# A two-layer kernel (depthwise-separable convolution, then a spiral scan): the pointwise product as three fp32r products, taken in the tick of the 512-wide layer

## The chip, the cores and the metric

The kernel runs on one core of a Trainium2 chip. The metric is the device time of one execution in microseconds (us); lower is better. TensorE is called PE below, its weight loads PEld, VectorE DVE, ScalarE ACT, GpSimd POOL, SyncE SP. A row of the trace is one instruction or a group of them.

## The reference

`x` is 32 images of 56 x 56 positions with 256 channels, float32. Layer 0 is a depthwise 3 x 3 convolution with dilation 2 on relu(x), then a pointwise 256 x 256 product, with biases and a normalization. Layer 1 walks the positions on a spiral, in place, and needs both a position's own value and the mean of its neighbours.

```
h = relu(x)
h = depthwise_conv(h, dw_kernel, dilation 2) + dw_bias
h = h @ pw_kernel + pw_bias                       # 256 -> 256
g = h * inv + (beta - moving_mean * inv)          # inv = gamma / sqrt(var + eps)
for p in spiral:                                  # one after the other, in place
    u = concat(g[p], mean of the neighbours of p) # 512 wide
    y = tanh(u @ w1 + b1) @ w2 + b2               # hidden layer, 512 wide
    g[p] = g[p] + y * w_y
```

## The kernel before

The work has two parts in time. In the first (up to about 3170 us of the profiled execution) everything is computed that does not depend on the scan's results: the layer-0 value of every position, and for every position the part of `u @ w1` that needs layer 0 alone. Both are written to DRAM in the order of the scan (`s_x`, `s_pre`). In the second part the scan reads them back tile by tile, adds the terms of the scan, and stores the output. The change is in the first part.

The first part handles 112 rows (56 image rows, for each half of the 32 images). A row is 7 tiles of 128 (position, image) pairs, so there are 784 tiles. All engines follow one order written out by hand: a loop over ticks, one tile for each tick. The tick of a step is its constant plus the tile's number. Per tick, and modulo 7 for what is done once for a row:

- SP loads a row of `x` (896 KB).
- PE transposes it in two of the seven ticks (7 pieces of 128 x 128, L861). ACT applies relu into `relu_rows` (L563, twice a row) and does the centre tap into `dw_rows` (L552, twice for a pair of rows).
- DVE does the other eight taps (L676, in a regular row eight instructions of 128 x 1792), the sums of neighbours (L689, L702, L712), and the low parts `u_lo` of the split operand (L726, four for a row).
- The split: an operand is rounded to fp32r (`u_hi`, on ACT, L541, four for a row: own values and neighbour sums, for tiles 0 to 3 and 4 to 6) and the rest is kept in `u_lo`. The first two of the four 128-deep slices are the row's own `dw_rows` values, the other two the neighbour sums.
- PE does the pointwise product of a tile in plain fp32 from `dw_rows` with `pw` (L872: two matmuls of 256 columns, four instructions in the trace) into banks 6 and 7. Six ticks later (`HID_LAG`) it does the 512-wide layer of that tile: for each of four slices hi*hi, hi*lo, lo*hi (L888, L889, L890), twelve fp32r matmuls of 512 columns into banks 4 and 5.
- ACT copies the two results out, one tick after each (`eo` from the 512-wide layer, L517, then `xo`, L523), and at the end of the tick writes the bias into the bank just emptied (L572). The pointwise product accumulates on that bias, so PE waits for L572 ahead of the product of the next tile but one. `eo` and `xo` have four slots each: ACT waits until the transfer of four tiles before has landed.
- POOL issues two indirect transfers in a tick, one after the other: `s_x` (L458, 128 KB) and `s_pre` (L464, 256 KB).

At the end of the first part SP waits for the last of both transfers before it reads `s_pre` back. In the setup DVE folds the normalization into `pw` (L613) and `bias_all` (L617), and PE transposes `pw` for the merged weights.

## Time and profile before

| what | value |
| --- | --- |
| three runs | 4768.79, 4776.31, 4791.13 us (median 4776.31) |
| profiled execution, its own time | 4755.92 us |
| its span, first to last instruction | 4754.1 us |
| mean granted TensorE clock | 0.993 |
| busy share of the span | PE 94%, PEld 70%, DVE 84%, ACT 54%, POOL 72% |
| first part | up to about 3170 us |

Matmuls are pipelined and their ends are modelled: consecutive matmul rows overlap, so the time of one is read from the distance of the starts, and a busy PE is not PE at its peak. "issue" in a wait means that nothing shown by the profile was waited for. Spans on POOL are rough.

### The profile page before, as it was taken

What the parts mean: (1) busy time and instruction counts of PE and PEld (TensorE: products, weight loads), DVE (VectorE), ACT (ScalarE), POOL (GpSimd) and SP (SyncE); (2) the same over time, 40 slices, a digit from 0 to 9 for tenths busy, and PEclk for the clock granted to TensorE, in tenths of its full rate; (3) what the DMA queues carried; (4) which work ended last, traced back from release to release, by engine and by line L of the source; (5) the groups of instructions that cost most, each with busy time, mean ns of one, the idle gap of its engine ahead of it and who ended that gap; (6) DMA issues with size and microseconds to landing.
All of it is one profiled execution on the core that took longest, in us unless ns stands there. A gap on an engine that the chain in (4) does not pass through costs nothing.

```text
span 4754.1 us, 62034 instructions
## 1 busy us (share of the span) xinstructions
PE 4491.0 (94%) x19609; PEld 3350.7 (70%) x19609; DVE 3981.0 (84%) x5685; ACT 2551.0 (54%) x4523; POOL 3445.8 (72%) x2478
## 2 busy tenths in 40 slices
PE   4999999999999999999999999998888899999889
PEld 3888878888888888888878888864444445555556
DVE  7888888888888788888888888738888888898884
ACT  4566656666666666665656666444344444444552
POOL 1888888888887788888888888756666666665542
PEclk8999999999999999999999999999999999999999
DMA  4344444444444444444444444359999998888751
GB/s 101 124 139 134 133 134 140 132 135 138 131 138 138 129 138 134 131 142 131 132 132 140 132 136 130 151 178 318 303 299 320 296 301 291 287 273 256 209 176 51
DMA packets 394994, 835.52 MB, mean 176 GB/s; under 512 B 76848, under 2 KB 178480, under 8 KB 394544
## 3 DMA queue, kind: packets, MB, share of 16 engines
q1 hardware_dynamic: 249008, 417.52, 31.4%
q0 software_dynamic: 143408, 411.26, 23.2%
q8 instruction: 163, 2.67, 0.2%
q10 hardware_dynamic: 2256, 2.77, 0.2%
q14 instruction: 159, 1.30, 0.1%
HBM read 420.17 MB, written 425.85 MB: 178 GB/s over the span
## 4 chain that ended last, share of the span: by engine, by line
PE 61%; DVE 12%; issue 10%; ACT 7%; DMA 5%; POOL 4%; SPq 0%; DVEq 0%; POOLq 0%; ACTq 0%
PE psum L888 13%; PE psum L890 13%; PE psum L889 13%; PE psum L872 13%; DVE psum L752 5%; DMA out<-dw_rows 4%; DVE dw_rows L760 3%; ACT relu_rows L563 3%; POOL out L476 3%; PE psum L861 3%; PE psum L928 2%; PE psum L912 1%; PE psum L901 1%; DMA s_pre<-eo,wave_idx 1%; PE psum L919 1%
## 5 line engine op out<-in xcount | busy, mean ns | idle before, releaser
L676 DVE SCALAR_TENSOR_TENSOR dw_rows<-relu_rows,taps,dw_rows 128x1792 f32<-128x1792 f32 x872 | 1803.4, 2079 | 6.2 <-issue 5.2
L464 POOL DMA_INDIRECT s_pre<-eo,wave_idx x784 | 1327.0, 1693 | 249.7 <-issue 224.2
L458 POOL DMA_INDIRECT s_x<-xo,wave_idx x784 | 1215.2, 1550 | 377.5 <-issue 233.8
L476 POOL DMA_INDIRECT out<-dw_rows x897 | 899.8, 1003 | 677.2 <-issue 401.3
L888 PE MATMUL psum<-w_hi,u_hi 128*128 128x512 f32 x3136 | 1383.4, 441 | 0.0
L890 PE MATMUL psum<-w_hi,u_lo 128*128 128x512 f32 x3136 | 1231.8, 393 | 0.0
L889 PE MATMUL psum<-w_lo,u_hi 128*128 128x512 f32 x3136 | 1224.7, 391 | 0.0
L517 ACT ACTIVATE eo<-psum 128x512 f32<-128x512 f32 x784 | 468.1, 597 | 1218.6 <-PE psum L890 1160.9
L901 PE MATMUL psum<-dw_rows,ident 128*128 128x512 f32 x1666 | 885.0, 613 | 98.1 <-DVE near L752 74.7
L872 PE MATMUL psum<-pw,dw_rows 128*128 128x256 f32 x3136 | 818.8, 384 | 61.6 <-ACT psum L572 44.9
L581 ACT ACTIVATE psum<-psum 128x512 f32<-128x512 f32 x897 | 522.0, 582 | 545.8 <-PE psum L912 283.7
L752 DVE CUSTOM_DVE_ANT_0 psum<-psum,dw_rows,b_col 128x512 f32<-128x512 f32 x897 | 676.4, 754 | 112.8 <-ACT psum L581 106.4
L872 PEld LDWEIGHTS psum<-pw,dw_rows 128*128 128x128 f32 x3136 | 570.7, 190 | 183.1 <-issue 103.3
L890 PEld LDWEIGHTS psum<-w_hi,u_lo 128*128 128x128 f32 x3136 | 589.7, 188 | 137.9
L889 PEld LDWEIGHTS psum<-w_lo,u_hi 128*128 128x128 f32 x3136 | 592.2, 189 | 122.5
L888 PEld LDWEIGHTS psum<-w_hi,u_hi 128*128 128x128 f32 x3136 | 591.8, 189 | 117.9
L912 PE MATMUL psum<-u_hi 128*128 128x512 f32 x897 | 620.1, 691 | 43.1 <-ACT u_hi L590 33.7
L726 DVE TENSOR_TENSOR u_lo<-near,u_hi 128x1024 fp32r<-128x1024 f32 x224 | 243.7, 1088 | 384.6 <-ACT u_hi L541 257.3
L760 DVE SCALAR_TENSOR_TENSOR dw_rows<-dw_rows,near 128x256 f32<-128x256 f32 x897 | 434.0, 484 | 126.7 <-DMA out<-dw_rows 80.5
L901 PEld LDWEIGHTS psum<-dw_rows,ident 128*128 128x128 f32 x1666 | 269.0, 189 | 336.0 <-issue 317.0
L563 ACT ACTIVATE relu_rows<-psum 128x896 f32<-128x896 f32 x224 | 414.6, 1855 | 20.7 <-DMA dwb_c<-L_conv_dw_bias 10.6
L572 ACT ACTIVATE psum<-bias_all 128x256 f32<-128x256 f32 x782 | 332.5, 425 | 5.6
(90 smaller groups left out, 3913.6 us busy)
## 6 DMA issues: line engine op xcount, KB each, us to landing
dw_rows<-s_pre SPq DMA_DIRECT2D x615, 256.0 KB
x_tok<-x SPq DMA_DIRECT2D x112, 896.0 KB
dw_rows<-s_x SPq DMA_DIRECT2D x615, 128.0 KB
dw_rows<-s_pre SPq DMA_DIRECT2D x169, 192.0 KB
dw_rows<-s_x SPq DMA_DIRECT2D x169, 96.0 KB
out<-dw_rows POOLq DMA_INDIRECT x897
s_x<-xo,wave_idx POOLq DMA_INDIRECT x784
s_pre<-eo,wave_idx POOLq DMA_INDIRECT x784
```

Source lines behind the costliest of these rows:

```text
L458: pool.indirect_dma_start(s_x, bass.IndirectOffsetOnAxis(wave_idx[:, n:n + 1], 0), xo[:, n % XO_SLOTS, :], None, bounds_check=TILES * P - ...
L464: pool.indirect_dma_start(s_pre, bass.IndirectOffsetOnAxis(wave_idx[:, n:n + 1], 0), eo[:, n % EO_SLOTS, :], None, bounds_check=TILES * P - 1,
L476: pool.indirect_dma_start(out_rows, bass.IndirectOffsetOnAxis(store_idx[:, c:c + 1], 0), o_t[:, c % OUT_SLOTS, :], None, bounds_check=OUT_ ...
L676: dve.scalar_tensor_tensor(out=dst, in0=pair_rows(relu_rows, k + ky - 1, c, 2 * kx * NB), scalar=taps[:, c, 3 * ky + kx:3 * ky + kx + 1], ...
L752: dve.tensor_tensor_reduce(out=bank, in0=bank, in1=w2_row, scale=1.0, scalar=b2_col[:, 0:1], op0=ALU.mult, op1=ALU.add, accum_out=y_of(c)) ...
L760: dve.scalar_tensor_tensor(out=o_t[:, c % OUT_SLOTS, :], in0=wy_row, scalar=y_of(c), in1=x_t[:, c % XT_SLOTS, :], op0=ALU.mult, op1=ALU.ad ...
L872: last = pe.matmul(bank, dw_rows[:, R % D_SLOTS, c, NB + P * t:NB + P * (t + 1)], pw[:, c, :], start=False, stop=c == CK - 1, skip_group_c ...
L888: pe.matmul(bank, hi, w_hi[:, k, :], start=k == 0, stop=False)
L889: pe.matmul(bank, hi, w_lo[:, k, :], start=False, stop=False)
L890: last = pe.matmul(bank, lo, w_hi[:, k, :], start=False, stop=k == 2 * CK - 1)
L901: pe.matmul(psum[:, c % BANKS, :], ident[:, :], pre_t[:, c % PRE_SLOTS, :], start=True, stop=False).then_inc(passed, 1)
L912: pe.matmul(psum[:, c % BANKS, :], s_rows[:, part, :], v_sel[:, row, :], start=False, stop=True, skip_group_check=by_act(c)).then_inc(pre_ ...
```

## The change

- `pw` is split in the setup into `pw_hi` and `pw_lo` (two instructions on DVE). It is itself loaded into a part of the `relu_rows` ring that is not in use yet.
- The pointwise product takes the operands of the 512-wide layer: for the two slices that hold the row's own values, `u_hi`*`pw_hi`, `u_hi`*`pw_lo`, `u_lo`*`pw_hi`, six fp32r matmuls of 256 columns. Each stands behind the matmul of the 512-wide layer that has the same stationary operand, in the same tick; the two fp32 matmuls are gone.
- The pointwise product is thereby six ticks later. One constant, `TILE_LAG`, replaces `HID_LAG` on PE, ACT and POOL. The number of ticks is unchanged.
- Waits for `xp_ready` where `dw_rows` is freed become waits for `lo_ready`, since the product does not read `dw_rows` any more.

```diff
-                n = tick - ROW_AT
-                if 0 <= n < TILES1:
-                    R, t = divmod(n, T)
-                    pe.wait_ge(conv_step, conv_done_for(R // 2))
-                    pe.wait_ge(xp_filled, n + 1)
-                    bank = xp_bank(n)
-                    for c in range(CK):
-                        last = pe.matmul(bank, dw_rows[:, R % D_SLOTS, c, NB + P * t:NB + P * (t + 1)], pw[:, c, :],
-                                         start=False, stop=c == CK - 1, skip_group_check=True)
-                    last.then_inc(xp_ready, 1)
-
-                n = tick - ROW_AT - HID_LAG
+                n = tick - ROW_AT - TILE_LAG
                 if 0 <= n < TILES1:
...
                     pe.wait_ge(lo_ready, 4 * R + 2 * part + 2)
+                    pe.wait_ge(xp_filled, n + 1)
                     if n >= 2:
                         pe.wait_ge(hid_copied, n - 1)
-                    bank = psum[:, 4 + n % 2, :]
+                    hid, point = psum[:, 4 + n % 2, :], xp_bank(n)
                     for k in range(2 * CK):
                         hi, lo = u_hi[:, slot, k, at:at + P], u_lo[:, slot, k, at:at + P]
-                        pe.matmul(bank, hi, w_hi[:, k, :], start=k == 0, stop=False)
-                        pe.matmul(bank, hi, w_lo[:, k, :], start=False, stop=False)
-                        last = pe.matmul(bank, lo, w_hi[:, k, :], start=False, stop=k == 2 * CK - 1)
+                        pe.matmul(hid, hi, w_hi[:, k, :], start=k == 0, stop=False)
+                        if k < CK:
+                            pe.matmul(point, hi, pw_hi[:, k, :], start=False, stop=False, skip_group_check=True)
+                        pe.matmul(hid, hi, w_lo[:, k, :], start=False, stop=False)
+                        if k < CK:
+                            pe.matmul(point, hi, pw_lo[:, k, :], start=False, stop=False, skip_group_check=True)
+                        last = pe.matmul(hid, lo, w_hi[:, k, :], start=False, stop=k == 2 * CK - 1)
+                        if k < CK:
+                            last_point = pe.matmul(point, lo, pw_hi[:, k, :], start=False, stop=k == CK - 1,
+                                                   skip_group_check=True)
+                    last_point.then_inc(xp_ready, 1)
                     last.then_inc(hid_ready, 1)
```

The rest of it, cut: on POOL and ACT the two blocks of a tick become one, with the order of the instructions kept.

```diff
 # POOL
-                n = tick - ROW_AT - 2
+                n = tick - ROW_AT - TILE_LAG - 2
                 if 0 <= n < TILES1:
                     pool.wait_ge(xp_copied, n + 1)
...
-                n = tick - ROW_AT - HID_LAG - 2
-                if 0 <= n < TILES1:
                     pool.wait_ge(hid_copied, n + 1)
 # ACT, centre tap
-                        act.wait_ge(xp_ready, 2 * T * (k - 2))
                         act.wait_ge(lo_ready, 4 * 2 * (k - 2))
 # DVE, setup
             link(dve.tensor_copy(bias_all[:, :], cst))
             assert done[0] == SETUP_CST
+            link(dve.tensor_copy(pw_hi[:, :, :], pw))
+            link(dve.tensor_tensor(pw_lo[:, :, :], pw, pw_hi[:, :, :].bitcast(f32), ALU.subtract))
 # SP and DVE, end of the first part
-            sp.wait_ge(xp_ready, TILES1)
+            sp.wait_ge(lo_ready, 4 * ROWS)
-            dve.wait_ge(xp_ready, TILES1)
+            dve.wait_ge(lo_ready, 4 * ROWS)
```

## Rows read from the trace of the kernel before

**Rows 1.** The page's busy time, and two stretches (busy us and instructions of PE, PEld, DVE, ACT, POOL; PEclk, DMA).
```profile
PE 4491.0 (94%) x19609; PEld 3350.7 (70%) x19609; DVE 3981.0 (84%) x5685; ACT 2551.0 (54%) x4523; POOL 3445.8 (72%) x2478
...
160.00:460.00 300.00, 297.91 (x1386) 246.43 (x1385) 265.56 (x166) 182.81 (x308) 253.05 (x155) 1.00 0.43 135
...
2560.00:2860.00 300.00, 297.94 (x1386) 246.42 (x1385) 265.46 (x166) 185.91 (x309) 250.84 (x154) 1.00 0.43 135
```

**Rows 2.** Groups of instructions, 460 to 2860 us (busy, mean ns; idle before, releasers).
```profile
L464 POOL DMA_INDIRECT s_pre<-eo,wave_idx x613 | 1065.6, 1738 | 190.5 <-issue 174.5 <-ACT xo L523 16.0
L458 POOL DMA_INDIRECT s_x<-xo,wave_idx x614 | 935.8, 1524 | 208.7 <-issue 187.4 <-ACT xo L523 20.8 <-ACT eo L517 0.6
L889 PEld LDWEIGHTS psum<-w_lo,u_hi 128*128 128x128 f32 x2448 | 461.8, 189 | 95.3
L517 ACT ACTIVATE eo<-psum 128x512 f32<-128x512 f32 x612 | 365.4, 597 | 927.4 <-PE psum L890 893.9 <-DMA s_pre<-eo,wave_idx 32.2 <-issue 0.6
```

**Rows 3.** Timeline of PE, ticks of the steady part (start, duration).
```profile
514.38 1.03 PE L872 MATMUL psum<-pw,dw_rows 128*128 128x256 f32 x4
517.99 1.02 PE L872 MATMUL psum<-pw,dw_rows 128*128 128x256 f32 x4
521.95 1.10 PE L872 MATMUL psum<-pw,dw_rows 128*128 128x256 f32 x4 [0.17 <-ACT psum L572]
```

**Rows 4.** Timeline of ACT, one regular row of 7 tiles, from tick to tick.
```profile
1428.56 0.60 ACT L517 ACTIVATE eo<-psum 128x512 f32<-128x512 f32 x1
1448.62 0.84 ACT L541 ACTIVATE u_hi<-dw_rows 128x768 fp32r<-128x768 f32 x1
1452.24 0.60 ACT L517 ACTIVATE eo<-psum 128x512 f32<-128x512 f32 x1 [2.50 <-PE psum L890]
1455.87 0.60 ACT L517 ACTIVATE eo<-psum 128x512 f32<-128x512 f32 x1
```

**Rows 5.** Timeline of PE and ACT at the end of the first part.
```profile
3134.96 1.02 PE L872 MATMUL psum<-pw,dw_rows 128*128 128x256 f32 x4
3138.59 1.02 PE L872 MATMUL psum<-pw,dw_rows 128*128 128x256 f32 x4
3166.89 0.60 ACT L517 ACTIVATE eo<-psum 128x512 f32<-128x512 f32 x1 [2.12 <-PE psum L890]
3169.61 0.60 ACT L517 ACTIVATE eo<-psum 128x512 f32<-128x512 f32 x1 [2.12 <-PE psum L890]
```

**Rows 6.** Timeline of PE in the scan: short fp32 matmuls, two instructions each.
```profile
4506.57 0.38 PE L919 MATMUL psum<-ident,near 128*124 128x128 f32 x2
4506.79 0.38 PE L920 MATMUL psum<-near 128*124 128x128 f32 x2
```

**Rows 7.** Timeline of DVE, the same row.
```profile
1446.09 1.23 DVE L726 TENSOR_TENSOR u_lo<-near,u_hi 128x1024 fp32r<-128x1024 f32 x1 [2.80 <-issue]
1449.50 0.96 DVE L726 TENSOR_TENSOR u_lo<-dw_rows,u_hi 128x768 fp32r<-128x768 f32 x1 [0.19 <-ACT u_hi L541]
1450.38 4.13 DVE L676 SCALAR_TENSOR_TENSOR dw_rows<-relu_rows,taps,dw_rows 128x1792 f32<-128x1792 f32 x2
1455.30 2.07 DVE L676 SCALAR_TENSOR_TENSOR dw_rows<-relu_rows,taps,dw_rows 128x1792 f32<-128x1792 f32 x1
```

**Rows 8.** Timeline of POOL beside it.
```profile
1444.44 0.98 POOL L458 DMA_INDIRECT s_x<-xo,wave_idx  x1 [0.31 <-issue]
1445.73 0.97 POOL L464 DMA_INDIRECT s_pre<-eo,wave_idx  x1 [0.30 <-issue]
1450.46 0.97 POOL L458 DMA_INDIRECT s_x<-xo,wave_idx  x1 [0.30 <-issue]
1455.66 2.56 POOL L464 DMA_INDIRECT s_pre<-eo,wave_idx  x1 [0.30 <-issue]
```

**Rows 9.** Timeline of DVE (setup) and POOL (last transfer of the first part).
```profile
38.58 0.42 DVE L620 COPY eo<-psum 128x256 f32<-128x256 f32 x1 [2.13 <-PE psum L823]
3170.98 0.97 POOL L464 DMA_INDIRECT s_pre<-eo,wave_idx  x1 [1.74 <-ACT eo L517]
```

More of the change, by code:

```diff
@@ L33 @@
 ROW_AT = 21
-HID_LAG = 6
+TILE_LAG = 6
 FIRST_TICK = -20
@@ L38 @@
 TILES1 = ROWS * T
-LAST_TICK = TILES1 - 1 + ROW_AT + HID_LAG + 3
+LAST_TICK = TILES1 - 1 + ROW_AT + TILE_LAG + 3
 CONV_TAPS = [(0, 0), (0, 1), (0, 2), (1, 0), (1, 2), (2, 0), (2, 1), (2, 2)]
@@ L268, in build @@
         w_lo = sb("w_lo", [P, 2 * CK, HID], f32r)
-        pw = sb("pw", [P, CK, C])
+        pw_hi = sb("pw_hi", [P, CK, C], f32r)
+        pw_lo = sb("pw_lo", [P, CK, C], f32r)
         ident = sb("ident", [P, P])
@@ L333, in build @@
         tmp_r = u_hi[:, 0, 0:2, :]
+        pw = relu_rows[:, R_SLOTS - 1, :, PADX * NB:PADX * NB + C]
         x_in = [sem(f"x_in{i}") for i in range(X_SLOTS)]
@@ L486, in _ @@
                 (mva, bc(mvar, C)), (gam, bc(gamma, C)),
-                (pw[:, :, :], pwk.rearrange("a b (k p) n -> p (a b k) n", p=P)),
+                (pw, pwk.rearrange("a b (k p) n -> p (a b k) n", p=P)),
                 (pwb_r, bc(pwb, C)), (mme, bc(mmean, C)), (bet, bc(beta, C)), (wy_s, bc(wy, C)),
@@ L511, in _ @@
                         act.activation(xp_bank(n), bias_all[:, :], ACT.Copy).then_inc(xp_filled, 1)
-                n = tick - ROW_AT - HID_LAG - 1
+                n = tick - ROW_AT - TILE_LAG - 1
                 if 0 <= n < TILES1:
@@ L517, in _ @@
                     act.activation(eo[:, n % EO_SLOTS, :], psum[:, 4 + n % 2, :], ACT.Copy).then_inc(hid_copied, 1)
-                n = tick - ROW_AT - 1
-                if 0 <= n < TILES1:
                     act.wait_ge(xp_ready, n + 1)
@@ L566, in _ @@
                                    ACT.Relu).then_inc(row_ready, 1)
-                n = tick - ROW_AT - 1
+                n = tick - ROW_AT - TILE_LAG - 1
                 if 0 <= n < TILES1 - XP_BANKS:
@@ L863, in _ @@
                     last.then_inc(x_transposed, 1)
-                n = tick - ROW_AT
-                if 0 <= n < TILES1:
-                    R, t = divmod(n, T)
-                    pe.wait_ge(conv_step, conv_done_for(R // 2))
-                    pe.wait_ge(xp_filled, n + 1)
-                    bank = xp_bank(n)
-                    for c in range(CK):
-                        last = pe.matmul(bank, dw_rows[:, R % D_SLOTS, c, NB + P * t:NB + P * (t + 1)], pw[:, c, :],
-                                         start=False, stop=c == CK - 1, skip_group_check=True)
-                    last.then_inc(xp_ready, 1)
-                n = tick - ROW_AT - HID_LAG
+                n = tick - ROW_AT - TILE_LAG
                 if 0 <= n < TILES1:
@@ L984 @@
 SETUP_CST = 1 + 6 + CK + 3 + 1
-SETUP_T = SETUP_CST + 4
+SETUP_T = SETUP_CST + 2 + 4
 SETUP_W = SETUP_T + 2 * CK
```

## The prediction

> **What bounds the kernel now.** The page comes first: PE is busy 94% of the span; in the first part, 784 ticks of one tile each, where the change lies, it is busy 298 of every 300 us at full granted clock [rows 1]. Two views are then needed, because matmul rows overlap and the busy share says little.
>
> The timeline of PE gives the tick from start to start of the pointwise product: 3.61 us (514.38 to 517.99), then 3.96 with a short wait for ACT's bias write L572 [rows 3]. ACT's copies show the whole row of 7 tiles: 1428.56 to 1455.87, 27.31 us [rows 4]. Every row has it: a row has 7 x (12 + 4) + 14 = 126 matmul instructions, and the first and the last of eight stretches of 300 us (two of the others are a little short) have 1386 of them, 11.0 rows [rows 1]. Apart from the start and the last four rows that makes about 105. Of the seven ticks, two carry transposes on top, and one is set by ACT: from L517 at 1452.24 ACT does its copies, an L541, the relu and the bias write without a pause and reaches the next L517 3.63 us later [rows 4], while PE waits. The other six are PE's own.
>
> The groups of instructions show a second engine that the busy share hides. From 460 to 2860 us POOL's two transfers take 1065.6 + 935.8 us, and 174.5 + 187.4 us more are the fixed 0.30 us between two of them; on ACT it waits some 37 us [rows 2]. So POOL is occupied 98.5% of 2400 us: it is as close to the limit as PE. ACT in turn waits 32.2 us for landed `s_pre` transfers, that is, POOL already pushes back at times [rows 2].
>
> Why POOL takes that long is read by laying its timeline beside DVE's. A transfer takes 0.97 us where it starts while DVE is idle or has started within 0.08 us (1445.73; 1450.46 against L676 at 1450.38), and otherwise ends 0.85 us after the DVE instruction that runs: 1455.66 + 2.56 = 1458.22, and the L676 of 1455.30 ended at 1457.37 [rows 7, 8]. [...]
>
> **The change part by part.** *PE.* At the end of the first part ticks with the pointwise product take 3.63 us (3134.96 to 3138.59), those without it 2.72 (3166.89 to 3169.61) [rows 5]. So the fp32 pair costs 0.91. The six new matmuls: 2.72 / 12 = 0.227 us for 512 columns, half for 256, 0.113; times six 0.68. A bound from below: short fp32 instructions, each with a weight load of its own, follow each other at 0.22 / 2 = 0.11 [rows 6], six make 0.66. From above: a load row lasts 0.189 [rows 2], and if a short matmul can't hide it, six cost 1.13. I take 0.113, because in rows 6 a load of this length stands behind a matmul as short as these. Gain 0.91 - 0.68 = 0.23 a tick.
>
> [...]
>
> On PE alone: six ticks of a row at 0.23 make 1.4 us (the tick that ACT sets gives nothing), 27.3 to 25.9.
>
> *POOL.* It still has 14 transfers in a row, and gets no faster. Count what DVE allows now. A row has ten instructions of about 2 us (eight L676, L689, L702), four L726 and the short L712. With 0.30 + 0.97 between two transfers, each of the ten lets through one, ending 0.85 behind it; so does the L726 that ends DVE's long wait. An L726 of 0.96 is passed over, except the one with 0.19 us of idle time ahead (the transfer at 1450.46). The long wait of 2.80 lets two through freely (1444.44, 1445.73). Sum 10 + 1 + 1 + 2 = 14, exactly what a row needs [rows 7, 8]. If PE is faster, it is these waits of DVE that shrink, because DVE's own work stays. How far? The second free transfer starts 0.85 + 0.30 + 0.97 + 0.30 = 2.4 us after the end of the last instruction, and the one after it, 1.27 later, must find the L726 of 1.23 us still running: 3.7 - 1.2 = 2.5. So 2.80 can become about 2.5. After that POOL falls behind, the four slots fill, ACT waits for a landed transfer, and PE and DVE wait for ACT. This gives 0.3 us of a row; the small wait can lend a few hundredths too, so I take 0.35: row 26.95, 105 x 0.35 = 37 us.
>
> *Ends.* Rows 108 to 111, without convolution on DVE, are PE's: 7 x 0.23 x 4 = 6 us gained. The last six ticks now carry the pointwise product: 6 x 0.68 = 4 lost. The last `s_pre` stood 1.37 us behind its `eo` (3169.61 to 3170.98 [rows 5, 9]); now an `s_x` of 0.30 + 0.97 and a part of the copy of `xo` come between, some 1.6 lost. The two DVE instructions of the setup, at most 2 x 0.42 each by the 256-column copy, fall into the 2.13 us that DVE waits there for PE [rows 9]; without that cover they cost 1.7. ACT's and SP's changed waits are for counters that are reached earlier. Together about 0.
>
> *Moved steps.* Six ticks later for the product moves L523, L572 and `s_x` too, but in ACT and POOL the order within a tick and the number are as before, so nothing new queues behind them. PE's wait for the bias stood at the head of a tick and still does.
>
> Sum: 4755.92 - 37 = 4719. The median of the runs shown, 4776.31, is 20 us above the profiled execution; predicted 4739.
>
> **Rivals.** *POOL doesn't bind* (transfers find gaps that my count misses): the row goes to 25.9 to 26.2, 1.1 to 1.4 x 105 = 115 to 147 us, on the median's base 4630 to 4660. For it: a wait of DVE of only 0.19 us ahead of a short L726 buys a whole transfer [rows 7, 8], and there are two such L726 in a row; against it: the 98.5%.
>
> *POOL's rate is the row.* Neither of the two waits lends anything; what PE gains, ACT waits for landed transfers. 4776, at most 15 less.
>
> *POOL loses a slot: slower.* The 0.19 us ahead of the L726 at 1449.50 come from ACT's L541 of the next tick, at 1448.62 [rows 4, 7], which follows PE. If PE's tick is 0.23 shorter, this wait is gone, the transfer at 1450.46 is blocked for the rest of an L676, and a row has 13. The fourteenth needs 1.27 us more of DVE idle time in the long wait: 2.5 + 1.27 = 3.8 for 2.8, less the 0.19, row 27.3 + 0.8 = 28.1, 0.8 x 105 = 84 us more, 4860. It decides as soon as the tick gains more than 0.19. Against it: once ACT waits for transfers, its ticks are apart again and the small wait returns by itself.
>
> [...]
>
> **How the numbers follow.** A difference under about 0.5% (24 us) can't be told from none in a measurement of this kernel. Forecast, row 26.6 to 27.07: 0.36. POOL doesn't bind: 0.20. POOL's rate is the row: 0.24. Lost slot: 0.16. Not short: 0.04. Faster 0.56, same 0.24, slower 0.20. The range leaves out the last case and a part of the outer two: 4640 to 4840. The forecast's own range is 4700 to 4750.
>
> **What would show it.** In the changed kernel: matmul rows of 256 columns 0.11 us ahead of the next (right) or 0.19 and more (not short). Ticks of 3.4 us on PE where nothing waits. The row between two L517 seven ticks apart: 26.95; 25.9 if POOL doesn't bind; 28.1 if it lost a slot. L517 waiting for `s_pre` in nearly every row, with POOL's wait for ACT gone, is the mark of POOL as the bound; L517 waiting for PE throughout would make the forecast wrong. DVE's long wait at 2.5, and whether the small one ahead of the 128x768 L726 is still there, tells forecast from lost slot.

## The result and the profile after

The changed kernel takes 4832.89 us (median; 4829.29 to 4835.48), the kernel before beside it 4777.1: a ratio of 1.0113 with an interval of [1.0091, 1.0134]. It is slower, where the prediction forecast 4739. The profiled execution has a span of 4833.7 us (before: 4754.1), 1.7% more. That is more than the medians give, because the kernel before was slower in its timed executions here (4768.79 to 4791.13) than in its profiled one (4755.92). Beside the experiments below its median is 4747.12 to 4763.51. So ratios of different experiments can be off against each other by about 0.6%, and where it matters the rows of the profiles are compared too. One execution of the grouped kernel below took 12346.51 us at a granted clock of 0.365; it is not in its ratio.

First the page's busy time, then the view of stretches: the same two as in [rows 1], with 460 to 2860 us between them (columns as there).

```profile
PE 4424.6 (92%) x21177; PEld 3342.9 (69%) x21177; DVE 3981.3 (82%) x5687; ACT 2541.5 (53%) x4523; POOL 3511.5 (73%) x2478
...
160.00:460.00 300.00, 285.23 (x1502) 239.70 (x1501) 261.64 (x164) 176.97 (x300) 252.87 (x151) 0.98 0.42 132
2560.00:2860.00 300.00, 285.17 (x1489) 240.50 (x1488) 256.03 (x160) 178.09 (x301) 252.42 (x152) 0.97 0.42 134
460.00:2860.00 2400.00, 2281.93 (x11998) 1921.75 (x11997) 2048.90 (x1274) 1432.35 (x2402) 2017.12 (x1202) 0.98 0.42 132
```

PE has less to do and is idle more: 285 us busy in 300, where it had 298. Its granted clock, 1.00 before, is 0.97 to 0.98 in these stretches. POOL issues 1202 transfers in 2400 us, before 1227: one each 2.00 us for 1.96. A tile needs two, so that is the row, 2% longer.

The groups of instructions between 460 and 2860 us answer [rows 2].

```profile
L464 POOL DMA_INDIRECT s_pre<-eo,wave_idx x601 | 1025.1, 1706 | 185.0 <-issue 164.6 <-ACT xo L521 15.2 <-ACT eo L517 5.2
L460 POOL DMA_INDIRECT s_x<-xo,wave_idx x601 | 992.5, 1651 | 198.2 <-issue 169.8 <-ACT xo L521 25.3 <-ACT eo L517 3.0
L878 PE MATMUL psum<-w_hi,u_hi 128*128 128x512 f32 x2401 | 980.3, 408 | 118.1 <-ACT psum L569 69.2 <-DVE u_lo L725 35.1 <-issue 13.3
L517 ACT ACTIVATE eo<-psum 128x512 f32<-128x512 f32 x600 | 359.6, 599 | 963.6 <-PE psum L884 722.0 <-DMA s_pre<-eo,wave_idx 224.8 <-issue 12.9
```

ACT waits 224.8 us for landed `s_pre` transfers (32.2 before): POOL is now what the first part waits for. Its transfers haven't become dearer by themselves: `s_pre` has a mean of 1706 ns (1738 before), `s_x` 1651 (1524), and a transfer with no DVE instruction beside it takes 0.97 us as before. But more of them take over 2 us, each beside a DVE instruction of 2 us: 193 of 1201, before 178 of 1226.

The mean hides what a row is. Measured from one copy of `xo` to the one seven tiles later, the row before was 27.3 us in 99 of 102 rows, with 14 transfers issued in nearly every one. In the changed kernel 57 of 102 rows take 26.4 us, with 12 or 13 transfers (12.8 on average), and 29 rows take 29 to 33 us, with 15 to 18. The mean is 28.01 (27.43 before, which includes two long rows of 32.6 and 33.9); 102 x 0.58 = 59 us, and the first instruction of the scan on DVE stands at 3250.85 for 3183.41. The scan itself gives 12 us more (1583 for 1571 us); the same scan takes anything from 1559 to 1576 us in the other kernels below, so most of that need not come from the change.

**Where the transfer goes.** In the kernel before the small wait ahead of the 128x768 low part has two lengths in turn, 0.19 us [rows 7] and, in the row beside it, 0.35:

```profile
1422.35 0.96 DVE L726 TENSOR_TENSOR u_lo<-dw_rows,u_hi 128x768 fp32r<-128x768 f32 x1 [0.35 <-ACT u_hi L541]
```

DVE's low parts L725 (L726 before), two neighbouring rows of 26.4 us:

```profile
1396.07 0.96 DVE L725 TENSOR_TENSOR u_lo<-dw_rows,u_hi 128x768 fp32r<-128x768 f32 x1 [0.35 <-ACT u_hi L539]
1396.94 4.08 DVE L675 SCALAR_TENSOR_TENSOR dw_rows<-relu_rows,taps,dw_rows 128x1792 f32<-128x1792 f32 x2
...
1418.90 1.22 DVE L725 TENSOR_TENSOR u_lo<-near,u_hi 128x1024 fp32r<-128x1024 f32 x1 [1.90 <-ACT u_hi L539]
1422.17 0.96 DVE L725 TENSOR_TENSOR u_lo<-dw_rows,u_hi 128x768 fp32r<-128x768 f32 x1
1423.05 4.07 DVE L675 SCALAR_TENSOR_TENSOR dw_rows<-relu_rows,taps,dw_rows 128x1792 f32<-128x1792 f32 x2
```

and POOL beside them:

```profile
1396.87 1.00 POOL L460 DMA_INDIRECT s_x<-xo,wave_idx  x1 [0.30 <-issue]
...
1421.28 1.69 POOL L460 DMA_INDIRECT s_x<-xo,wave_idx  x1 [0.30 <-issue]
1423.27 2.70 POOL L464 DMA_INDIRECT s_pre<-eo,wave_idx  x1 [0.30 <-issue]
```

In the first row the low part waits 0.35 us and the transfer of 1396.87 gets through in 1.00. In the next its wait is only 0.05, too short to be shown, and there is no such transfer: the one of 1421.28 waits for the L675 before, and the next starts at 1423.27, 0.22 us after the L675 of 1423.05, and takes 2.70 us. Of 86 such low parts between 460 and 2860 us, 38 have a wait of under 0.1 us, mostly 0.05, and most others have 0.35; before, 87 of 88 had 0.19 or more. So one row of two has lost the transfer: counted from one 128x1024 low part of the neighbour sums to the next, rows of 26.4 us let through 12 with the short wait and 13 with the other. The long wait, 2.80 before, is 1.90 here: one transfer fits in freely (1418.16, 0.97), not two. That costs one transfer in every row, and the short small wait another in every second one. So a row lets through 12 or 13.

**What a stall looks like.** The missing transfers add up in the four slots until they are full. ACT, then PE:

```profile
296.61 0.60 ACT L517 ACTIVATE eo<-psum 128x512 f32<-128x512 f32 x1 [1.91 <-DMA s_pre<-eo,wave_idx]
304.10 0.60 ACT L517 ACTIVATE eo<-psum 128x512 f32<-128x512 f32 x1 [5.61 <-DMA s_pre<-eo,wave_idx]
313.97 0.60 ACT L517 ACTIVATE eo<-psum 128x512 f32<-128x512 f32 x1 [5.19 <-PE psum L884]
```
```profile
307.68 0.77 PE L878 MATMUL psum<-w_hi,u_hi 128*128 128x512 f32 x1 [3.91 <-ACT psum L569]
308.25 0.41 PE L880 MATMUL psum<-pw_hi,u_hi 128*128 128x256 f32 x1
308.46 0.63 PE L881 MATMUL psum<-w_lo,u_hi 128*128 128x512 f32 x1
308.88 0.41 PE L883 MATMUL psum<-pw_lo,u_hi 128*128 128x256 f32 x1
```

PE stands still for 3.91 us and then starts its matmuls at twice the distance (0.42 for 512 columns, 0.21 for 256). The stretches around it show the clock (columns as above):

```profile
300.00:307.00 7.00, 3.77 (x20) 2.86 (x18) 4.46 (x4) 2.90 (x4) 5.47 (x6) 0.96 0.74 230
307.00:313.00 6.00, 5.32 (x16) 4.48 (x17) 6.00 (x4) 1.75 (x5) 5.39 (x3) 0.50 0.24 87
```

The granted clock goes down inside the idle time: 1.00 up to 306 us, 0.69 from 306 to 307, 0.50 from 307 to 312.94, 0.90 from 313 to 314 and 1.00 again after.

### The profile page after: what moved, and what is told of

Same layout as the page of the kernel before. It is cut to its first block, busy times and chain, and to the rows that moved or that the text cites. A ratio compares the mean times of both kernels' runs of the same rounds, so it can differ in the third digit from the quotient of the medians.

```text
span 4833.7 us, 64390 instructions
## 1 busy us (share of the span) xinstructions
PE 4424.6 (92%) x21177; PEld 3342.9 (69%) x21177; DVE 3981.3 (82%) x5687; ACT 2541.5 (53%) x4523; POOL 3511.5 (73%) x2478
## 4 chain that ended last, share of the span: by engine, by line
PE 48%; issue 15%; DVE 14%; POOL 9%; DMA 8%; ACT 5%; SPq 0%; another core or an unknown queue 0%; POOLq 0%; DVEq 0%; ACTq 0%
PE psum L878 10%; PE psum L884 10%; PE psum L881 10%; DVE psum L751 4%; DMA s_pre<-eo,wave_idx 4%; DMA out<-dw_rows 4%; POOL s_x L460 3%; DVE dw_rows L759 3%; POOL out L476 3%; DVE dw_rows L675 3%; PE psum L886 3%; POOL s_pre L464 3%; PE psum L883 3%; PE psum L880 2%; PE psum L899 2%
## 5 line engine op out<-in xcount | busy, mean ns | idle before, releaser
L675 DVE SCALAR_TENSOR_TENSOR dw_rows<-relu_rows,taps,dw_rows 128x1792 f32<-128x1792 f32 x872 | 1802.6, 2078 | 6.0 <-issue 5.0
L460 POOL DMA_INDIRECT s_x<-xo,wave_idx x784 | 1277.6, 1630 | 388.7 <-issue 232.3
L878 PE MATMUL psum<-w_hi,u_hi 128*128 128x512 f32 x3136 | 1279.0, 408 | 191.8 <-ACT psum L569 90.2
L884 PE MATMUL psum<-w_hi,u_lo 128*128 128x512 f32 x3136 | 1252.0, 399 | 0.0
L881 PE MATMUL psum<-w_lo,u_hi 128*128 128x512 f32 x3136 | 1245.0, 397 | 0.0
L725 DVE TENSOR_TENSOR u_lo<-near,u_hi 128x1024 fp32r<-128x1024 f32 x224 | 244.5, 1091 | 441.7 <-ACT u_hi L539 357.4
L886 PE MATMUL psum<-pw_hi,u_lo 128*128 128x256 f32 x1568 | 446.6, 285 | 0.0
L883 PE MATMUL psum<-pw_lo,u_hi 128*128 128x256 f32 x1568 | 444.2, 283 | 0.0
L880 PE MATMUL psum<-pw_hi,u_hi 128*128 128x256 f32 x1568 | 442.6, 282 | 0.0
```

Of the source, the lines that this page charges most:

```text
L460: pool.indirect_dma_start(s_x, bass.IndirectOffsetOnAxis(wave_idx[:, n:n + 1], 0), xo[:, n % XO_SLOTS, :], None, bounds_check=TILES * P - ...
L675: dve.scalar_tensor_tensor(out=dst, in0=pair_rows(relu_rows, k + ky - 1, c, 2 * kx * NB), scalar=taps[:, c, 3 * ky + kx:3 * ky + kx + 1], ...
L878: pe.matmul(hid, hi, w_hi[:, k, :], start=k == 0, stop=False)
L881: pe.matmul(hid, hi, w_lo[:, k, :], start=False, stop=False)
L883: pe.matmul(point, hi, pw_lo[:, k, :], start=False, stop=False, skip_group_check=True)
L884: last = pe.matmul(hid, lo, w_hi[:, k, :], start=False, stop=k == 2 * CK - 1)
```

## The experiments

The theory (A): POOL's transfers are clocked by DVE's instructions, the small wait ahead of a 128x768 low part is worth a whole transfer, and a shorter tick of PE removes it. The rivals: the six products cost PE more than the pair did, the moved step costs something by itself, or transfers collide with the loads of `x` in the DMA engines. The recorded expectations call their rivals B and C anew each time; A is the same in all. The line numbers below are those of each kernel.

**One extra product in a tick.** The tick is brought back by one 256-column matmul.

```diff
+                    last_point = pe.matmul(psum[:, 6 + n % XP_BANKS, C:2 * C], lo, pw_hi[:, 1, :], start=False,
+                                           stop=True, skip_group_check=True)
                     last_point.then_inc(xp_ready, 1)
```

> The changed kernel with one more 256-column fp32r product a tick, into a half of the bank that nobody reads; it leaves nothing out. Theory A (POOL's slots: with PE's tick at 3.47 us instead of 3.62, DVE has too little idle time for POOL's 14 transfers of a row, 12 to 13 get through, and every third or fourth row is long because ACT waits for a slot): the extra product of 0.12 us makes the tick 3.59, the rows go back to 27.1 to 27.3 us with 14 transfers each and no long ones, and the kernel is FASTER with more work: 4760 to 4790 us. Theory C (the moved or interleaved product itself costs): 784 x 0.12 = 94 us more than the changed kernel, about 4925.

Measured: 1.017 [1.0149, 1.0192], 4828.35 for 4747.12. Rows of 26.97 us with 12 to 14 transfers (13.3 on average), ACT's wait for `s_pre` 196.9 us, mean row 28.04. The rows of 27.1 to 27.3 us with 14 transfers that A expected did not come, nor did the 94 us of products that simply add up: the mean row is that of the changed kernel. In 38 of 86 low parts the small wait is 0.09 to 0.19 us, too short for the profile to show in the line below (the L675 before ends at 1418.65), and too short for the transfer:

```profile
1416.58 2.07 DVE L675 SCALAR_TENSOR_TENSOR dw_rows<-relu_rows,taps,dw_rows 128x1792 f32<-128x1792 f32 x1
1418.78 0.96 DVE L725 TENSOR_TENSOR u_lo<-dw_rows,u_hi 128x768 fp32r<-128x768 f32 x1
1419.66 4.07 DVE L675 SCALAR_TENSOR_TENSOR dw_rows<-relu_rows,taps,dw_rows 128x1792 f32<-128x1792 f32 x2
```
```profile
1419.80 2.79 POOL L464 DMA_INDIRECT s_pre<-eo,wave_idx  x1 [0.30 <-issue]
```

The transfer starts 0.14 us after the L675 and is held; with the wait of 0.19 it started 0.08 after and got through. The wait and this distance add up to about 0.27 us in each of these rows, so 0.19 was only just enough. This run alone doesn't separate A from products that cost PE more than the pair did.

**Two extra products**, the same line twice.

> The changed kernel with two more 256-column products a tick into the unread half of the bank (nothing left out). One extra product made rows of 26.97 us (7 x 0.08 over 26.41) and still 12 to 14 transfers a row: the small wait of DVE ahead of the 128x768 L725 was gone in every second row. Theory A (that wait decides): two make the row 27.5, the wait is back at 0.2 or more in every row, 14 transfers a row, no long rows; total 0.2 x 105 = 20 us over the kernel with the moved fp32 pair, a ratio of 1.000 to 1.004 to the kernel before, FASTER than the changed kernel (1.011) and than the one with one extra product (1.017). Theory C (extra PE work simply adds): 1.025 to 1.03.

Measured: 1.0045 [1.0028, 1.0062]. Every row is 27.7 us with 14 transfers, the small wait (0.24 to 0.35) is in every row, the long one is 3.2, and ACT waits 26.4 us for `s_pre`. The row was expected at 27.5 and the ratio at 1.004 at most, so both are just above. With 512 more columns on PE in each tile than the changed kernel it is the faster of the two (1.0045 against 1.0113, mean row 27.70 against 28.01). If the products themselves made the loss, it would have to be the slowest. The row of 27.7 is PE's own: the granted clock is 1.00 and PE is busy in all of the 2400 us:

```profile
460.00:2860.00 2400.00, 2400.00 (x13343) 2076.33 (x13343) 2072.13 (x1289) 1454.11 (x2426) 2015.05 (x1215) 1.00 0.43 134
```

**The moved step alone**, with the old fp32 pair on `u_hi` in the new place.

```diff
+                    for c in range(CK):
+                        last_point = pe.matmul(point, u_hi[:, slot, c, at:at + P].bitcast(f32), pw_hi[:, c, :].bitcast(f32),
+                                               start=False, stop=c == CK - 1, skip_group_check=True)
-                        if k < CK:
-                            pe.matmul(point, hi, pw_hi[:, k, :], start=False, stop=False, skip_group_check=True)
```

> One part of the change alone: the product stands in the tick of the 512-wide layer as in the changed kernel, but as the two fp32 matmuls of before (on u_hi read as fp32; the low part of the operands is left out). Theory A: the tick is 3.63 as before, rows 27.3 us with 14 transfers, 4770 to 4790 us. Theory C (moving the product six ticks later costs, through ACT, POOL or the end of the first part): it stays at 4820 to 4840 us.

Measured: 0.9973 [0.9962, 0.9984]. All rows 27.3 us with 14 transfers, waits of 0.20 or 0.34 ahead of the low part, 16.3 us for `s_pre`. So the move costs nothing, and the loss comes with the six products in place of the pair. (The 4770 to 4790 us expected start from the slower base of the first measurement; its time is 4733.44, with 4747.12 for the kernel before beside it.)

**One transfer a tile** for both results (rows of 3 KB), so 7 transfers a row.

```diff
-                    pool.indirect_dma_start(s_x, bass.IndirectOffsetOnAxis(wave_idx[:, n:n + 1], 0),
-                                            xo[:, n % XO_SLOTS, :], None, bounds_check=TILES * P - 1,
...
-                    pool.indirect_dma_start(s_pre, bass.IndirectOffsetOnAxis(wave_idx[:, n:n + 1], 0),
-                                            eo[:, n % EO_SLOTS, :], None, bounds_check=TILES * P - 1,
+                    pool.indirect_dma_start(s_all, bass.IndirectOffsetOnAxis(wave_idx[:, n:n + 1], 0),
+                                            both[:, n % EO_SLOTS, :], None, bounds_check=TILES * P - 1,
```

> The changed kernel with one indirect transfer a tile in place of two: ACT writes both results side by side into one buffer, and rows of 3 KB go to one DRAM tensor, from which the scan reads its two parts. Theory A: POOL has 7 transfers a row instead of 14 and no longer binds, every row goes to PE's 26.4 us, 105 x 0.9 = 95 us less than before, 4670 to 4700 us. Theory B (not POOL's rate but the late landing of a transfer behind the load of a row of x makes the stalls of 5.6 us): the same landings, the same stalls, 4800 us or more.

> One transfer a tile as in e3_merged, but with the product as the two fp32 matmuls (the low part of its operands is left out). It splits the gain of e3_merged. Theory A: without the faster product PE's row is 27.3 us whatever POOL does, so ratio 0.995 to 0.999, as with the moved fp32 pair alone; the three products are worth 0.9 us x 105 = 95 us (2%), and only with POOL out of the way. If the merged transfer is the gain by itself: 0.98.

Measured: with the six products 0.9773 [0.9754, 0.9791], with the fp32 pair in the same place 0.9927 [0.9911, 0.9944]. Both are a little faster than expected (4641.99 us for 4670 to 4700; 0.9927 for 0.995 to 0.999). Once POOL has room, the change of products is a gain: 1.5% by the two ratios, which come from different measurements, and 1.9% by the profiled spans (4640.9 for 4730.1) and by the rows, 26.43 us for 27.3. POOL is busy 1025.1 of 2400 us with the six products. In this kernel ACT never waits for a transfer, and still 45 of 91 low parts have the short wait of 0.05 us; with 7 transfers a row nothing depends on it.

**The taps of DVE cut short**: each of the eight taps handles 64 elements instead of 1792.

> The changed kernel with DVE's taps cut to 64 columns of one channel block instead of 1792 (the rest of the depthwise convolution is left out). It tests what makes a transfer on POOL long. If it is the running DVE instruction: nearly all transfers take 0.97 us, POOL is never full, rows are PE's 26.4 us or a little less, total about 4660 to 4690. If POOL's time of 1.65 us a transfer is its own: it stays, and so does the total, 4830.

Measured, one execution: 4610.53 us, below the 4660 to 4690 expected. All rows 26.41 us with 14 transfers, twelve of them at 0.97 us. The same 14 transfers as in the changed kernel, with the same bytes, and no stall: it is DVE's long instructions that cost the transfers, not their number. (The row is that of the next kernel; of the 34 us by which the span is shorter, 20 lie ahead of the first copy of `eo`, 89.24 for 109.49.)

**Two useless instructions of DVE**, ahead of the two 128x768 low parts.

```diff
+                    if n >= 5:
+                        if 2 * R + n - 5:
+                            dve.wait_ge(padded, 2 * R + n - 5)
+                        dve.tensor_scalar(spare[:, :], v_rows[:, :], 1.0, None, ALU.mult).then_inc(padded, 1)
                     dve.wait_ge(hi_ready, 4 * R + n - 2)
```

> The changed kernel with two more instructions a row on DVE, of no use (128x512, about 0.34 us from start to start), ahead of the two 128x768 L725, before their wait. Theory A: with it the next L675 starts 1.1 us behind the end of the one before, so that a transfer of POOL gets through beside each of these two, in every row; with the ten long instructions, the awaited L725 and one more in the long wait (which shrinks to some 1.5 us) that makes 14 in PE's row of 26.4 us. Long rows vanish; ratio to the kernel before 0.975 to 0.985, more work on the busiest vector engine and yet 3% faster than the changed kernel. If POOL needs DVE's idle time as such, 0.7 us a row less of it makes the kernel slower than the changed one: 1.015 to 1.03.

Measured: 0.9762 [0.9745, 0.9778], 3.5% less than the changed kernel to which it only adds work (4.0% by the profiled spans). All rows 26.40 us with 14 transfers. DVE and POOL of this kernel:

```profile
1403.27 0.42 DVE L728 TENSOR_SCALAR spare<-v_rows 128x512 f32<-128x512 f32 x1
1403.60 0.95 DVE L731 TENSOR_TENSOR u_lo<-dw_rows,u_hi 128x768 fp32r<-128x768 f32 x1
1404.47 4.08 DVE L677 SCALAR_TENSOR_TENSOR dw_rows<-relu_rows,taps,dw_rows 128x1792 f32<-128x1792 f32 x2
1408.47 0.41 DVE L728 TENSOR_SCALAR spare<-v_rows 128x512 f32<-128x512 f32 x1
1408.81 0.95 DVE L731 TENSOR_TENSOR u_lo<-near,u_hi 128x768 fp32r<-128x768 f32 x1
1409.68 2.08 DVE L677 SCALAR_TENSOR_TENSOR dw_rows<-relu_rows,taps,dw_rows 128x1792 f32<-128x1792 f32 x1
```
```profile
1402.51 1.69 POOL L466 DMA_INDIRECT s_pre<-eo,wave_idx  x1 [0.30 <-issue]
1404.50 0.97 POOL L462 DMA_INDIRECT s_x<-xo,wave_idx  x1 [0.30 <-issue]
1405.78 1.63 POOL L466 DMA_INDIRECT s_pre<-eo,wave_idx  x1 [0.30 <-issue]
1407.71 1.69 POOL L462 DMA_INDIRECT s_x<-xo,wave_idx  x1 [0.30 <-issue]
1409.70 0.97 POOL L466 DMA_INDIRECT s_pre<-eo,wave_idx  x1 [0.30 <-issue]
```

Pad and low part together last 1.2 us (1403.27 to 1404.47), so a transfer that ended 0.93 us into them is followed by one that starts 0.03 us after the next L677 and gets through in 0.97. That happens twice in a row, at 1404.50 and at 1409.70.

**The kernel before with the same two pads.**

> The kernel BEFORE with the same two useless 128x512 instructions of DVE a row, ahead of the two 128x768 low parts. Theory of the slots: PE still sets rows of 27.3 us there, DVE's long wait shrinks from 2.8 to about 2.0, a row has at least 14 slots, so nothing changes: ratio 0.998 to 1.002, row 27.3. If the two instructions are good by themselves (whatever PE does, by spacing DVE's instructions or calming the transfers), this kernel gains too: ratio under 0.99.

Measured: 0.997 [0.9959, 0.998]. The row is 27.31 as before, while POOL's busy time falls to 1812.83 of 2400 us (2001.09 in the kernel before). Just outside the expected 0.998, like the moved step alone; that the two rare long rows of the kernel before are missing here (mean row 27.31 for 27.43, 12 us in 102 rows) and its shorter scan (1563 us for 1571) would explain it, which is not shown. The pads are worth 3.5% only where PE could go faster. It also shows that the row of the kernel before was set by PE and ACT, not by POOL, which was only just quick enough.

**Loads of `x` cut** to 64 of 1792 columns from the third row on.

> The changed kernel with the loads of x cut to 64 of 1792 columns from the third row on (the rest of x is stale, so the values are wrong). The transfer that ACT waits for longest lands 5.6 us after its issue, where others take under 2, and the load of a row of x runs at that time. Theory A (POOL's issue rate is the bound): rows of 26.4 us still get 12 to 13 transfers; late landings are gone, but the mean row stays near 28.0, with more and shorter waits; ratio 1.005 to 1.015. Theory B (the late landing makes the loss): no slot wait, all rows 26.4, ratio 0.977.

Measured: 1.0071 [1.0054, 1.0088], mean row 27.84. The late landings are gone: none of 604 `s_pre` transfers lands more than 4 us after its end, where 73 of 599 do in the changed kernel. Stalls remain, and ACT's wait for `s_pre` is even 355.5 us. In the kernel before 98 of 613 land as late, without a loss. The collision in the DMA engines is real, but it is not the cause: taking it away gives back 0.4 of the 1.1%.

**One pad** of DVE, ahead of the low part of the row's own values only (`if n == 5`).

> The changed kernel with ONE useless 128x512 instruction of DVE (0.42 us) a row, ahead of the 128x768 low part of the row's own values; the kernel with two of them (one ahead of each 128x768 low part) has rows of 26.40 us with 14 transfers in each. By the count of transfers a row now has ten long instructions of DVE, the 128x1024 low part that ends the long wait, the fixed pause, and two in the long wait: 14, as the prediction's forecast wanted, and the long wait may shrink to 2.5 us. DVE's own work in a row is 26.40 - 2 x 0.42 - 1.6 (its long wait there) = 23.96 us, so the row is 23.96 + 0.42 + 2.5 = 26.9 us, the low parts find a gap in every row, nothing alternates, and the ratio to the kernel before is about 1 - 0.41 x 104 / 4754 = 0.991 (0.987 to 0.995). If one pad does what two do (all that matters is that rows don't alternate), the row is 26.4 and the ratio 0.976. If a pad only helps because DVE is held up by 0.84 us in all, rows alternate still and the ratio is above 1.005.

Measured: 1.0051 [1.0032, 1.0071], outside the 0.987 to 0.995. The pad takes the place of the small wait in every row, but the rows don't settle at 26.9: 81 of 102 take 26.4 us, most with 13 transfers, and 21 take 31.5 to 33. The long wait is 1.9 us where 2.5 was expected. POOL falls behind by one transfer a row, and every fourth to fifth row pays for it. Mean row 27.61 = 26.4 + 1.2. From this came the rule that the two grouped kernels at the end were forecast with: row = free row + 1.27 us for each transfer short of 14.

**Products grouped** behind the twelve matmuls of the 512-wide layer instead of interleaved; first with one transfer a tile.

```diff
                     for k in range(2 * CK):
                         hi, lo = u_hi[:, slot, k, at:at + P], u_lo[:, slot, k, at:at + P]
                         pe.matmul(hid, hi, w_hi[:, k, :], start=k == 0, stop=False)
-                        if k < CK:
-                            pe.matmul(point, hi, pw_hi[:, k, :], start=False, stop=False, skip_group_check=True)
...
+                    for k in range(CK):
+                        hi, lo = u_hi[:, slot, k, at:at + P], u_lo[:, slot, k, at:at + P]
+                        pe.matmul(point, hi, pw_hi[:, k, :], start=False, stop=False, skip_group_check=True)
```

> The changed kernel with one transfer a tile (rows of 3 KB for both results, 7 transfers a row instead of 14), and the six 256-column products grouped behind the twelve matmuls of the 512-wide layer instead of interleaved with them. If the place among the twelve is indifferent for PE, as distances of 0.117 and 0.23 us in both places would say, the ratio is that of the merged kernel with interleaved products, 0.9773, within 0.003 (0.974 to 0.981), and a tick of PE where nothing waits is 3.47 us. If sharing a stationary operand with the neighbour is worth something, the tick is longer by up to six weight loads that are no longer beside their own, at most 6 x (0.189 - 0.117) = 0.43 us, and the ratio is up to 1.0.

Measured: 0.9608 [0.959, 0.9625], 4565.21 us, the fastest of all and outside both expectations. PE's tick is 3.46 us grouped and 3.48 interleaved where nothing waits; what changes is ACT. Its copies with grouped products:

```profile
1420.40 0.60 ACT L511 ACTIVATE both<-psum 128x512 f32<-128x512 f32 x1 [2.12 <-PE psum L871]
1422.13 1.85 ACT L552 ACTIVATE relu_rows<-psum 128x896 f32<-128x896 f32 x1
1424.16 0.61 ACT L511 ACTIVATE both<-psum 128x512 f32<-128x512 f32 x1
1427.38 0.60 ACT L511 ACTIVATE both<-psum 128x512 f32<-128x512 f32 x1 [1.93 <-PE psum L871]
```

and with interleaved ones:

```profile
1416.18 0.60 ACT L511 ACTIVATE both<-psum 128x512 f32<-128x512 f32 x1 [0.58 <-PE psum L876]
1419.97 0.59 ACT L511 ACTIVATE both<-psum 128x512 f32<-128x512 f32 x1
1423.89 0.60 ACT L511 ACTIVATE both<-psum 128x512 f32<-128x512 f32 x1 [2.05 <-PE psum L876]
```

Grouped, the 512-wide result is finished 0.7 us before the end of the tick, and ACT copies it while PE does the short products. Its crowded tick of 3.76 us (1420.40 to 1424.16) is made good in the next one, 3.22. Interleaved, the last matmul of the 512-wide layer is also the last of the tick, and the crowded ticks of ACT (3.79 for 3.48) stay in the row: 26.43 against 25.83.

**Grouped, with two transfers a tile**, without and with the two pads.

> The changed kernel, two transfers a tile, with the six short products grouped behind the twelve matmuls of the 512-wide layer instead of interleaved. With one transfer a tile this edit alone takes the row from 26.43 to 25.83 us (ratio 0.9773 to 0.9608), because the 512-wide result is ready 0.7 us before the end of the tick and ACT has that much more time. The rule that the runs so far suggest: row = free row + 1.27 us for each transfer short of 14, where the free row is what PE and ACT allow and the number let through in a free row is counted on DVE. It gives 26.4 + 1.27 = 27.67 for the kernel with one pad (measured 27.61, 13 in each free row) and 26.4 + 1.5 x 1.27 = 28.3 for the changed kernel (measured 28.01; 12 and 13 alternate). Here: free row 25.83, 12.5 let through as there, so 25.83 + 1.9 = 27.7, and the ratio is about 1 + (27.7 - 27.43) x 102 / 4754 = 1.006 (1.002 to 1.010): slower than the kernel before though PE and ACT could do a row 1.5 us faster. If grouping gives its 0.6 us a row whatever POOL does, the same number by chance (1.0113 - 0.013 = 0.998), and free rows of 25.83 with the same stalls; if DVE's shorter wait loses a further transfer, 1.03.

> The same grouped kernel with the two useless 128x512 instructions of DVE a row. Interleaved, with the two pads, the rows were 26.40 with 14 transfers and a long wait of 1.6 us (ratio 0.9762). Grouped, a free row is 25.83, and DVE's long wait shrinks to 25.83 - 23.96 - 0.84 = about 1.0 us or a little less. A transfer ends 0.85 us into that wait, the next could start at 1.15 and finds the low part of 1.23 us running already: it ends 0.85 behind it instead of 0.97 after its start, and one of the 14 is lost. So: free rows of 25.83 with 13 transfers and a stalled one every few rows, mean 25.83 + 1.27 = 27.1, ratio about 0.993 (0.989 to 0.998): slower than the interleaved kernel with the same pads by 1.5 to 2%, although its free row is 0.6 us shorter. If the theory of slots is wrong here and faster PE and ACT are simply faster, the ratio is 0.9762 - 0.0145 = 0.962.

Measured: 1.0103 [1.0074, 1.0133] without pads, just above the 1.002 to 1.010 expected, mean row 27.92; with pads 0.9965 [0.9952, 0.9977], mean row 27.17 for the 27.1 expected. The second is the sharper test: its free rows are 25.85 us where the interleaved kernel with the same pads has 26.40, and it is 2% slower, because its long wait of 1.0 us loses the transfer that 1.6 us let through:

```profile
1442.44 1.23 DVE L731 TENSOR_TENSOR u_lo<-near,u_hi 128x1024 fp32r<-128x1024 f32 x1 [0.97 <-ACT u_hi L541]
...
1468.32 1.23 DVE L731 TENSOR_TENSOR u_lo<-near,u_hi 128x1024 fp32r<-128x1024 f32 x1 [1.10 <-ACT u_hi L541]
...
1494.18 1.23 DVE L731 TENSOR_TENSOR u_lo<-near,u_hi 128x1024 fp32r<-128x1024 f32 x1 [4.87 <-ACT u_hi L541]
```

(the third stands in a stalled row). The kernels with two transfers a tile together, 102 rows each; the free row is the short one that most rows have, and the number is the mean of the transfers issued in those:

| kernel | free row, us | transfers in it | free + 1.27 x (14 - transfers) | mean row | ratio |
| --- | --- | --- | --- | --- | --- |
| before | 27.3 | 14.0 | 27.3 | 27.43 | 1 |
| before, two pads | 27.3 | 14.0 | 27.3 | 27.31 | 0.997 |
| after | 26.4 | 12.8 | 27.9 | 28.01 | 1.0113 |
| one extra product | 27.0 | 13.3 | 27.9 | 28.04 | 1.017 |
| two extra products | 27.7 | 14.0 | 27.7 | 27.70 | 1.0045 |
| two pads | 26.4 | 14.0 | 26.4 | 26.41 | 0.9762 |
| one pad | 26.4 | 13.2 | 27.4 | 27.61 | 1.0051 |
| grouped | 25.85 | 12.6 | 27.6 | 27.92 | 1.0103 |
| grouped, two pads | 25.85 | 13.35 | 26.7 | 27.17 | 0.9965 |

The rule was made after the kernel with one pad, so only the two grouped lines test it. It is good to 0.5 us, always on the low side when transfers are missing: the free rows counted include some just behind a stall, which have 14. With the 13 of the others the last line is 27.1. That a stall costs more than its transfers (late landings, the lower clock) is possible and not separated.

## Why the prediction was wrong

*The mechanism was seen, and its outcome was judged wrongly.* That POOL is as close to the limit as PE, that its transfers follow the ends of DVE's instructions, that a row has exactly 14 slots and that the wait of 0.19 us holds one of them: all of it held. The lost-slot rival (row 28.1, 4860, with a chance of 0.16) names what happened: the mean row is 28.01. That its size fits so well is partly luck. It had every row at 28.1 with a long wait of 3.8 us; the trace has rows of 26.4 us and stalled ones. The wide range of 4640 to 4840 holds the 4832.89 us only because it takes in a part of this rival.

*The step that failed* is "So 2.80 can become about 2.5. After that POOL falls behind, the four slots fill, ACT waits for a landed transfer, and PE and DVE wait for ACT", read as a point at which the row settles. It doesn't settle. With four slots between them PE and ACT run on at their own 26.4 us for rows, the long wait is 1.9 us or so and not 2.5, the row lacks one or two transfers, and then one long row pays for several. The one-pad kernel was forecast with the same step, and missed for the same reason.

*The argument against the rival failed too*: "once ACT waits for transfers, its ticks are apart again and the small wait returns by itself". The wait stands at 0.35 us in about half of the rows, but not because ACT waits: with one transfer a tile ACT never waits for a transfer, and the short wait stands in the same half of the rows (45 of 91). The prediction looked at one row and took its 0.19 for all. The two lengths in turn, 0.19 and 0.35, have become 0.05 and 0.35. Only the first of them loses its transfer, which makes 12.5 a row and not 12.

*The gain of the tick* was mis-sized: 0.23 forecast, 0.14 measured. Where nothing waits, the tick is 3.48 us in the trace for 3.61 to 3.63 before. The 512-column matmuls follow each other at 0.230 in the steady part, where 0.227 came from the last ticks, so the fp32 pair was worth some 0.86 and not 0.91; the short ones follow at 0.117, where 0.113 was taken. Six ticks at 0.14 are 0.84 us, most of the way from 27.3 to the 26.4 of the free row. The rival's own limit, "as soon as the tick gains more than 0.19", was much too high. The wait need not vanish: 0.19 us was about the least that lets the transfer through, so one extra product, which leaves a gain of about 0.04, still lost it in half of the rows. Two extra ones, with a tick longer than before, kept it in all.

*PE's side otherwise held.* Short products are short: they follow each other at 0.117 us, although each has a load row of 0.19 us (192 to 193 ns on average for L880, L883 and L886). So "not short", with its chance of 0.04 and its 0.19 and more, did not come; nor do the load rows of 0.19 us (190 to 191 ns) hold up the 512-column matmuls, 0.230 us apart. "POOL doesn't bind" named 25.9 to 26.2 for the row; with one transfer a tile it is 26.43 interleaved and 25.83 grouped. The tick that ACT sets was counted as giving nothing, which the grouped order shows to be a matter of the order of the matmuls.

*The moved step, the setup and the ends* were put at about nothing; the moved step alone is 0.9973. (From 160 to 2860 us there are nine stretches of 300 us and not eight; nothing hangs on it.)

## What to carry to other kernels

Where POOL issues transfers beside long instructions of DVE, count how many transfers DVE's gaps let through in one period, and compare with the number needed: the busy share of POOL doesn't tell it (2001 of 2400 us with 14 transfers a row before, 2017 with 12.8 in most rows after). If the two are equal, making another engine faster can close a gap of a few tenths of a microsecond and cost a whole transfer (1.27 us here); first take transfers away (one for two gave 3 to 5%) or place a gap on purpose, then speed up PE. The four buffers between two engines did not soften the shortage here, they turned it into rare long stalls, so look at single periods and not at means. And where two results leave PE in one tick, finish first the one with the longer way ahead of it (rows of 25.83 us for 26.43 here).

## What the runs showed of the hardware

- A transfer issued by POOL takes 0.97 us where no DVE instruction runs (103 of them in the kernel before between 460 and 2860 us, 0.967 to 0.982). It also took 0.97 when it started up to 0.08 us after a DVE instruction of 2 us (1450.46 against 1450.38 [rows 7, 8]; 1404.50 against 1404.47 with two pads); started 0.09 to 0.4 us after, it took 2.54 to 2.84 (2.79 at 0.14 us with one extra product, 2.70 at 0.22 in the changed kernel). In ten of the kernels with two transfers a tile (before, changed, one and two extra products, moved fp32 pair, two pads, one pad, before with two pads, grouped, grouped with two pads; 460 to 2860 us) 531 transfers that started beside a DVE instruction of 2 us got through in 0.97 to 0.98 us, the last at 0.084 us after its start; 1602 that started up to 0.4 us after it were held, one of them at 0.064 us and all others at 0.084 or later. With one transfer a tile four were held that started only 0.001 to 0.006 us after (2.86 to 2.89 us). A held transfer ended 0.85 us after the DVE instruction (medians of 0.846 to 0.849 in the ten kernels).
- The DVE instructions were not held in turn. In the changed kernel, between 460 and 2860 us, the L675 that start 0.04 to 0.14 us after a transfer take 2.08 us (58 of them), like the 124 that start with no transfer under way.
- In the changed kernel an `s_pre` transfer issued at 296.84 to 298.53 had landed only when ACT went on at 304.10, 5.57 us later; half of these transfers land within 1.75 us of their end, and 152 of 599 take over 2.5. The load of a row of `x` (896 KB) ran on the DMA engines for 4.7 us of it (298.17 to 302.86), at a DMA share of 0.93 to 0.94 from 299 to 304 us.
- After 3.91 us without a matmul PE ran at a granted clock of 0.50 for 5.3 us (307.68 to 312.94 in the changed kernel), with 512-column matmuls 0.42 us apart.
- In the changed kernel matmuls of 256 and of 512 columns in fp32r, into two PSUM banks in turn, are followed by the next after 0.117 and 0.230 us; interleaving the two accumulations costs PE 0.02 us a tick (3.48 us for 3.46 grouped).
